# Delta rule of a three-part block: value columns ahead of gate columns, half of the decay factors made early

## The reference

```
qkv = x @ w_qkv;  z = x @ w_z;  beta = sigmoid(x @ w_b)
g = -exp(a_log) * softplus(x @ w_a + dt_bias)
qkv = silu(causal depthwise conv of 4 taps(qkv))     # q, k: 16 heads, v: 32 heads of 128
q, k = l2norm(q) * 128 ** -0.5, l2norm(k)
g = cumsum(g) within the chunk of 64
decay[i, j] = exp(g[i] - g[j]) for i >= j, else 0
A = -(beta * k) @ k.T * decay, strictly lower
attn = inverse(I - A);  v_new = attn @ (beta * v)
o = (q @ k.T * decay) @ v_new
out = (o * rsqrt(mean(o * o) + eps) * norm_w * silu(z)) @ w_out
```

## Time and profile before

| | us |
|---|---|
| median of 3 runs (lowest to highest) | 2776.75 (2775.61 to 2778.75) |
| the profiled execution, its own time | 2778.05 |
| its span | 2776.3 |
| projection columns 32 to 95 in it | 1970 to 2194 |
| groups in it | 2194 to 2362 |

### The profile page before, as it was taken

The page is one execution under the profiler, slowest core; times in us unless marked ns, Lnnn a source line. Parts: engine busy times, 40 slices in busy tenths (PEclk is TensorE's granted clock), DMA queues, the critical chain, the costliest instruction groups (busy, mean ns, idle before and its releaser), DMA issues.

```text
span 2776.3 us, 38769 instructions
## 1 busy us (share of the span) xinstructions
PE 2639.8 (95%) x13810; PEld 2192.9 (79%) x13810; DVE 1766.5 (64%) x3857; ACT 1529.8 (55%) x2992; POOL 502.1 (18%) x428
## 2 busy tenths in 40 slices
PE   6879999999999999999999999999999879998999
PEld 5668788888887887887887887878777669777887
DVE  7855636546546546546455466668669866668997
ACT  7944435435435435445444355437686567856776
POOL 4402102002002012011011020015353332022111
PEclk9989999999999999999999999999999999999999
DMA  3533013022022021030030121435675642549996
GB/s 126 137 98 104 18 43 104 11 61 85 15 77 65 20 85 49 24 94 30 27 100 16 40 85 48 149 123 162 171 214 168 155 95 67 187 186 366 377 372 226
DMA packets 255054, 317.85 MB, mean 114 GB/s; under 512 B 128712, under 2 KB 166216, under 8 KB 241808
## 3 DMA queue, kind: packets, MB, share of 16 engines
q1 hardware_dynamic: 251392, 310.03, 35.3%
q0 software_dynamic: 3040, 5.08, 0.7%
q10 hardware_dynamic: 432, 0.27, 0.0%
HBM read 274.22 MB, written 46.98 MB: 116 GB/s over the span
## 4 chain that ended last, share of the span: by engine, by line
PE 80%; DVE 10%; ACT 3%; DMA 2%; issue 2%; SPq 1%; POOL 1%; POOLq 0%; DVEq 0%; ACTq 0%
PE ps L103 21%; PE ps L105 21%; PE ps L104 21%; PE ps L887 3%; PE ps L843 3%; PE ps L915 2%; DVE lnw L2171 2%; DVE zz L2174 2%; PE ps L868 2%; DVE cv L2138 1%; PE ps L908 1%; PE ps L1346 1%; PE ps L1345 1%; PE ps L2012 1%; ACT qn L380 1%
## 5 line engine op out<-in xcount | busy, mean ns | idle before, releaser
L1246 POOL TENSOR_TENSOR lnw<-lnw,half 128x8 f32<-128x8 f32 x88 | 144.4, 1641 | 1202.4 <-DVE lnw L981 1202.4
L103 PE MATMUL ps<-whf,cth 128*128 128x512 f32 (+1 forms) x832 | 335.9, 404 | 0.0
L103 PE MATMUL ps<-cnh,pth 128*128 128x512 f32 (+1 forms) x832 | 330.1, 397 | 1.4 <-issue 1.4
L105 PE MATMUL ps<-whf,ctl 128*128 128x512 f32 (+1 forms) x832 | 325.9, 392 | 0.0
L104 PE MATMUL ps<-wlf,cth 128*128 128x512 f32 (+1 forms) x832 | 325.5, 391 | 0.0
L104 PE MATMUL ps<-cnl,pth 128*128 128x512 f32 (+1 forms) x832 | 324.9, 390 | 0.0
L105 PE MATMUL ps<-cnh,ptl 128*128 128x512 f32 (+1 forms) x832 | 324.7, 390 | 0.0
L2664 DVE TENSOR_TENSOR ml<-mr,mh 128x2048 fp32r<-128x2048 f32 x90 | 203.3, 2287 | 26.6 <-ACT mh L2606 26.6
L1157 ACT ACTIVATE pr<-ps,sm 128x1601 f32<-128x1601 f32 x56 | 89.7, 1601 | 210.0 <-DVE sm L1023 210.0
L1182 ACT ACTIVATE xo<-ps 128x128 f32<-128x128 f32 x64 | 17.8, 278 | 312.7 <-PE ps L915 312.7
L1042 DVE TENSOR_TENSOR ptl<-ps,pth 128x512 fp32r<-128x512 f32 (+1 forms) x256 | 139.1, 585 | 79.0 <-ACT pth L1169 78.6
(11 more groups left out here) (352 smaller groups left out, 6398.4 us busy)
## 6 DMA issues: line engine op xcount, KB each, us to landing
mr<-in_moe SPq DMA_DIRECT2D x90, 1024.0 KB, 7.0
ctr<-in_ctxt SPq DMA_DIRECT2D x96, 256.0 KB, 2.7
pr<-in_ctxn SPq DMA_DIRECT2D x96, 256.0 KB
wv<-in_wv SPq DMA_DIRECT2D x64, 256.0 KB, 2.8
wr<-in_wqkv SPq DMA_DIRECT2D x64, 256.0 KB, 2.9
wvf<-in_wattn SPq DMA_DIRECT2D x11, 1024.0 KB, 5.1
ca<-cat_d SPq DMA_DIRECT2D x16, 512.0 KB, 3.9
qk_d<-cv SPq DMA_DIRECT2D x32, 256.0 KB, 3.2
```

The source lines that it names most:

```text
L103: pe.matmul(dst, lh, rh, start=first, stop=False)
L105: return pe.matmul(dst, ll, rh, start=False, stop=last)
L1246: po.tensor_tensor(rs[0:w, s, :], nv[0:w, s, :], half[0:w, 0:8], ALU.pow).then_inc(kx_rs, 1)
```

## The change

Columns 32 to 63 are now all values and columns 64 to 95 all gates. The decay factors of builds 16 to 31 are made in four rounds among columns 54 to 89, each for 16 rows of the gate table: eight broadcast loads into the tile pg, mask and gate added by GpSimd, one exponential, then products with beta and with the norm of q by GpSimd, and a store of both to cf_d. The loads of these builds fetch the factors, so their "build" has no step on GpSimd and no "decay", and "second" makes the coupling by two smaller products (L2243, L2245 of the changed kernel). Since the factors hold the norm, groups from 16 on are evicted without a scale. The gate table in DRAM has three planes (with the norm) and lies in halves. The first solve has larger budgets (columns 63 to 76), the second starts at 81 and ends by 93. The clearing of mt and xt moves from column 38 to 91, behind the last store of factors. Squares start at t = 8 at half the pace, with two per step from 24 on; those from group 8 on are one operation on ScalarE and a reduction on VectorE. Who evicts which group stays as it was.

```diff
-        gb_d = dram("gb_d", [128, 2, 128])
+        gb_d = dram("gb_d", [2, 128, 3, 64])
+        cf_d = dram("cf_d", [4, 128, 2048])
...
-        gT = sb5g("gT", [128, 2, 128])
+        gT = sb5g("gT", [128, 3, 128])
         s5g.close()
+        s5p = ExitStack()
+        pg = stack_sb(s5p)("pg", [128, 16, 3, 64])
+        s5p.close()
...
-        OUT_AC = 20
...
+        ALONE = 8
+
+        def on_ac(n):
+            return n < 20
...
-        GATE_PLACES, VALUE_PLACES, place = [], [], 32
-        for k in range(32):
-            if k not in (6, 12, 18, 24):
-                GATE_PLACES.append(place)
-                place += 1
-            VALUE_PLACES.append(place)
-            place += 1
-        GATE_PLACES += list(range(place, NPOS))
+        VALUE_PLACES, GATE_PLACES = list(range(32, 64)), list(range(64, NPOS))
...
-                yield "decay", n, 0
...
+                k, r = divmod(s - 54, 9)
+                if 0 <= k < 4:
+                    if r < 2:
+                        yield "pg_load", k, 2 * r
+                        yield "pg_load", k, 2 * r + 1
+                    if r in (3, 4):
+                        yield "pg_mask", k, r - 3
+                    if r == 5:
+                        yield "pg_exp", k, 0
+                    if r in (6, 7):
+                        yield "pg_scale", k, r - 6
+                    if r == 8:
+                        yield "pg_store", k, 0
+                if s == 91:
+                    yield "clear", 0, 0
...
-                if 63 <= s < 83:
-                    yield from some(steps, 170 if burst < 4 and 4 <= r < 8 else 800)
-                if s == 83:
+                if 63 <= s < 76:
+                    yield from some(steps, 600 if burst < 4 and 4 <= r < 8 else 1300)
+                if s == 76:
                     yield from steps
-                if s == 84:
                     yield "solved", 0, 0
+                if s == 79:
                     yield "system", 1, 0
                     steps = solving(1)
-                if 88 <= s < NPOS:
-                    yield from some(steps, 700 if s < 92 else 2000)
+                if 81 <= s < 93:
+                    yield from some(steps, 1100)
+                if s == 93:
+                    yield from steps
+                    yield "solved", 1, 0
...
-            squares, fetched, solved_to = 0, 3, 0
+            squares, fetched, solved_to = 0, 3, 1
             for t in range(36):
                 if t < 32:
                     yield "p0", t, 0
-                yield from some(steps, 400 if t < 3 else 700)
+                yield from some(steps, 500 if t < 12 else 700)
                 if 0 <= t - 1 < 32:
                     yield "p1", t - 1, 0
-                for _ in range(2 if t < 3 else 1):
+                for _ in range(2 if t < 4 else 1):
                     if todo:
                         yield from building(todo.pop(0))
-                if t == 13:
+                if t == 12:
                     yield from built()
                 if 0 <= t - 2 < 32:
                     yield "p2", t - 2, 0
-                yield from some(steps, 400 if t < 3 else 800 if t < 15 else 1000)
+                yield from some(steps, 400 if t < 12 else 800)
                 if 0 <= t - 3 < 32:
                     yield "p3", t - 3, 0
-                if t in (4, 14, 22):
+                if t in (14, 22):
                     yield from steps
-                    solved_to = (4, 14, 22).index(t) + 1
+                    solved_to = (14, 22).index(t) + 2
                     yield "solved", solved_to, 0
-                if t in (6, 15):
-                    steps = solving(2 if t == 6 else 3)
+                if t in (5, 16):
+                    steps = solving(2 if t == 5 else 3)
                 while fetched < 16 and 2 * fetched <= t + 3 and fetched // 4 <= solved_to:
                     yield "fetch", fetched, 0
                     fetched += 1
-                if t in (5, 14):
+                if t in (4, 14):
                     yield "system", solved_to + 1, 0
                 if t >= 2 and t % 2 == 0 and t // 2 + 1 < 16:
                     yield "fetch_coupling", t // 2 + 1, 0
-                if squares <= t - 4 and squares < 28:
-                    yield "square", squares, 0
-                    squares += 1
-                    if squares % 2 == 0:
-                        yield "rms", squares // 2 - 1, 0
+                for _ in range(2 if t >= 24 else 1 if 8 <= t and t % 2 == 0 else 0):
+                    if squares < 28:
+                        yield "square", squares, 0
+                        squares += 1
+                        if squares % 2 == 0:
+                            yield "rms", squares // 2 - 1, 0
...
+            if m >= 8:
+                sp.wait_ge(*d_cf.at(16 * ((m - 8) // 2 + 1)))
             for b in range(2):
-                sp.dma_start((gb2 if core_over(m) else gb)[64 * b:64 * b + 64, f:f + 2, :, :, :].rearrange("p f h a t -> p (f h) a t"),
-                             gb_d[8 * m:8 * m + 8, :, 64 * b:64 * b + 64].unsqueeze(0).to_broadcast([64, 8, 2, 64])).then_inc(d_gb[m % 4].sem, 16)
+                dst = (gb2 if core_over(m) else gb)[64 * b:64 * b + 64, f:f + 2, :, :, :]
+                if m >= 8:
+                    sp.dma_start(dst.rearrange("p f h a t -> p (f h a t)"),
+                                 cf_d[(m - 8) // 2, 64 * b:64 * b + 64, 1024 * (m % 2):1024 * (m % 2) + 1024]).then_inc(d_gb[m % 4].sem, 16)
+                else:
+                    sp.dma_start(dst.rearrange("p f h a t -> p (f h) (a t)"),
+                                 gb_d[b, 8 * m:8 * m + 8, 0:2, :].rearrange("h a t -> h (a t)").unsqueeze(0).to_broadcast([64, 8, 128])).then_inc(d_gb[m % 4].sem, 16)
+
+        def factor_load(sp, k, part):
+
+            sp.wait_ge(d_gt, 32)
+            if k > 0:
+                sp.wait_ge(*d_cf.at(16 * k))
+            h, row = 4 * part, 64 + 16 * k + 4 * part
+            for b in range(2):
+                sp.dma_start(pg[64 * b:64 * b + 64, h:h + 4, :, :].rearrange("p h a t -> p (h a t)"),
+                             gb_d[b, row:row + 4].rearrange("h a t -> (h a t)").unsqueeze(0).to_broadcast([64, 768])).then_inc(d_pg.sem, 16)
+
+        def factor_store(sp, k):
+            sp.wait_ge(*pg_scaled.at(4 * k + 4))
+            sp.dma_start(cf_d[k].rearrange("p (h c) -> p h c", h=16),
+                         pg[:, :, 0:2, :].rearrange("p h a t -> p h (a t)")).then_inc(d_cf.sem, 16)
...
-                    sp.dma_start(gb_d, gT[:, :, :]).then_inc(d_gt, 16)
+                    for b in range(2):
+                        sp.dma_start(gb_d[b], gT[:, :, 64 * b:64 * b + 64]).then_inc(d_gt, 16)
...
+                elif step == "pg_exp":
+                    ac.wait_ge(*pg_masked.at(8 * n + 8))
+                    ac.activation(pg[:, :, 0, :], pg[:, :, 0, :], ACT.Exp).then_inc(pg_exp.sem, 1)
...
+                    if n < 16:
+                        for q in range(4):
+                            f = ac.activation(vb[:, j, h + q, :], bank(3 + n % 5)[:, 128 * q:128 * q + 128], ACT.Copy,
+                                              scale=rq[:, j, h + q:h + q + 1])
+                    else:
+                        f = ac.activation(vb[:, j, h:h + 4, :], bank(3 + n % 5).rearrange("p (h d) -> p h d", h=4), ACT.Copy)
...
-                    ac.wait_ge(*apD_out.at(n + 1))
+                    ac.wait_ge(*group_out(n))
                     if n >= 3:
                         ac.wait_ge(*sso_out.at(n - 2))
                     else:
                         ac.wait_ge(*d_gz[n].at(16 * (11 if n < 2 else 10)))
-                    for h in range(4):
-                        hd = 4 * (n % 8) + h
-                        f = ac.activation(gz[:, n % 3, 128 * h:128 * h + 128], vb[:, n // 8, hd, :], ACT.Square,
-                                          accum_out=sso[:, n // 8, hd:hd + 1])
-                    f.then_inc(sso_out.sem, 1)
+                    hd = 4 * (n % 8)
+                    if n < ALONE:
+                        for h in range(4):
+                            f = ac.activation(gz[:, n % 3, 128 * h:128 * h + 128], vb[:, n // 8, hd + h, :], ACT.Square,
+                                              accum_out=sso[:, n // 8, hd + h:hd + h + 1])
+                        f.then_inc(sso_out.sem, 1)
+                    else:
+                        ac.activation(gz[:, n % 3, :].rearrange("p (h d) -> p h d", h=4), vb[:, n // 8, hd:hd + 4, :],
+                                      ACT.Square).then_inc(o_squared.sem, 1)
...
-                elif step == "start":
-                    po.wait_ge(d_gt, 16)
+                elif step == "pg_mask":
+                    e = pg[:, 8 * k:8 * k + 8, 0, :]
+                    po.wait_ge(*d_pg.at(128 * (n + 1)))
+                    po.tensor_tensor(e, e, negm.unsqueeze(1).to_broadcast([128, 8, 64]), ALU.add).then_inc(pg_masked.sem, 2)
+                    m = 4 * n + 2 * k
```

(42 more changed lines are left out.)

36 lines of the change are left out of this document (24 added, 12 removed).

## The result

The changed kernel takes **2808.5 us** (median of 4 runs, 2806.8 to 2810.9) against 2776.2 for the kernel before on the same chip (2774.0 to 2778.8, 4 runs): ratio 1.0120, 95% interval 1.0108 to 1.0133. It is slower by 1.2%; the forecast was 2769 with a range up to 2786. The profiled execution took 2809.1 us with a span of 2807.3. Three executions of the experiments' sets that took 5240 to 9297 us are left out of the ratios.

What follows compares the result with a forecast made beforehand. VectorE was taken to bound the stretches where TensorE waits. Groups starting 14 us later and 21 us removed from them gave -7 on 2778.05, 2771; less 1.3 and rounding, 2769, range 2750 to 2786.

Steps and rivals of the forecast that it cites:

- Value part, +2: Value columns 32 to 63: VectorE keeps up, ScalarE comes near TensorE's pace; 2 us, from 0 to 6.
- Order and VectorE's load, columns to 2187 without locks and seam: Gate columns: two solves, splits, taps and `second`s on VectorE make TensorE wait 9 us beyond 2176.
- floor of 2176: End of the columns if TensorE waits for nothing, from the present 2194.1 less waits and lower-clock time.
- Locks, +18: Gate columns: 28.2 us of GpSimd work beside two solves holds VectorE up at 0.65, 18 us, all reaching TensorE.
- Rivals 1 and 2: GpSimd's rounds don't block VectorE, 2751, chance 0.24; or all 28.2 us of GpSimd are lost to VectorE, 2779, chance 0.12.
- The transfers, +0: Columns: the forecast's sum has no term for the bytes that the factor rounds move.
- rival 3: Columns: SyncE's queue bounds, factor loads waiting for the former round's store, chunk loads behind: +15, 2784, chance 0.14.
- Seam, +3: Columns to groups: clearing mt and xt waits for the last factor store, delaying fetch and eviction; 3 us, 0 to 6.
- Groups, -21: Delta rule groups: second solve gone, less GpSimd and ScalarE work, fewer waits and less low clock; 21 us removed.
- The fetch of the fourth system 1.2 becomes 2: Groups: TensorE's wait at the fetch of the fourth solved system grows from 1.2 to 2 us.
- Rival 4: Groups give little, as TensorE waits for chains of latencies: 15 us less gained, 2784, chance 0.05; sign, over 160 us.

Runs made afterwards that it cites:

- order alone: Kernel before with only the new column order and the first two solves' new budgets, no factor rounds: 2782.2 us, ratio 1.0014 to 1.0036.
- six slots: Changed kernel with six slots instead of three for the gate columns' results, three of them in cv: 2808.6 us, ratio 1.0103 to 1.0137.

## Why the prediction was wrong

The direction, the size and the range all failed: 2769 forecast, 2808.5 measured. The step that failed most is one term that was put at nothing, the bytes of the factor rounds; the order of columns, the seam and the groups were mis-sized as well. By its steps:

- **Value part, +2.** Right: TensorE was idle 3.3 of its 115 us, and ScalarE, which was to come near TensorE's pace, busy 99.4.
- **Order and VectorE's load, columns to 2187 without locks and seam.** The order alone came to 2198.7, 12 us later. TensorE was idle 18.0 us in its columns from 1970 on (228.0 less 209.95 busy) where the prediction's 9 and 2 make 11. Some 4 of the rest are in the floor of 2176, which leaves 206 us for TensorE's own work where it was busy 210. The forecast had a gain of 7 from the new distribution; it cost 5.
- **Locks, +18.** Right in kind and near in size: VectorE lost some 17 us in the gate columns, at an estimated 0.65 per us of GpSimd as forecast, and the columns 12.3, or 15.8 with the transfers out of the way (352.2 less 336.4). Rivals 1 and 2 are both out.
- **The transfers, +0.** This is the step that failed. "Against: where VectorE lags, SyncE is not the last" dismissed rival 3 by asking who comes last in SyncE's queue. The runs showed 13.8 us for the bytes of three rounds, or 17.3 with GpSimd's work out of the way (353.7 less 336.4); the stands themselves, rival 3's mechanism, gave 3.3 back when removed. The sum of bytes per column was never made, though the prediction's own rows have the column times. Rival 3 let 1.6 MB move in 3 us, which is over 500 GB/s, where no stretch of the columns shown here moved more than 303. It also let a chunk load be some 8 us late, though each waits for one of three slots first. The rings of gz and wr then turn late landings into late high parts.
- **Seam, +3.** 5.9 us at the first p0, at the upper end of the 0 to 6 it was given; the order alone had 0.8 there.
- **Groups, -21.** 9.6 measured. Up to the 24th group the forecast held: the 21st p0 came 95.0 us after the first, before 112.9, so 17.9 less, and the 24th 106.5, before 126.9. "The fetch of the fourth system 1.2 becomes 2" was 6.9; at the 25th group 13.2 were left. But the fetch alone is not the cause, as the solves made earlier took that wait away and gave back 0.7. The last stretch gave back 3.6 more, 2.8 of it because TensorE was busy 37.6 us with the 308 matmuls it does there in place of 34.8, at a granted clock of 0.95 in place of 1.00. Rival 4 (over 160 us) is out by 2 us only, less than the 5 by which the groups scatter.

In the sum, the columns lost 38.7 against 14 forecast: 12 of the difference are the order's, some 14 the transfers', 2 to 3 the seam, with the locks 2 to 6 under the forecast. The groups add 11. That these parts come so near the whole is in part luck, as the locks and the transfers each come out 3.5 us dearer when the other is out of the way. Against the order alone, the factors cost 33.3 us in the columns and gave 9.0 back in the groups (166.8 less 157.8); even at the 21st group they were ahead by only 17.2 (112.2 less 95.0).

What stays open: how the 12 us of the order's shortfall divide between splits made too late and the gz ring, as the six slots took only 2.4 of them; whether the rounds' bytes cost by rate or by later landings; what of the groups' gain is the factors', and why the earlier solves gave nothing; and whether the factors' volume would be cheaper in another form, which wasn't tried.

## What to carry to other kernels

Before gathering columns of one kind, add up the bytes per us that they want from the DMA engines, with every store and every new transfer, and compare it with the mixture before (here some 299 against 133 GB/s). Then ask how many slots each transfer has: here, with three, landings later by 1 to 2 us came with longer waits of the engines. A high share of the DMA engines is not yet a loss; the changed kernel's last stage had 1.00 with TensorE busy 70.0 of 70 us. The longest pieces of the chain of waits name what was last, not what is dear; only the kernel without the wait tells (here 3.3 us for 14.5% of the chain). The same holds for a single wait of TensorE: taking 6.7 us of it away gave 0.7. And widening one ring may only uncover the next.

## What the runs showed of the hardware

- VectorE's operations on two SBUF tiles lost about 0.65 us (an estimate from the two traces) for each us of GpSimd operations taken away, 24 operations of 512 elements; the mean of a 128x512 split rose from 724 to 927 ns.
- In 2110 to 2200 us of the change, with a share of the DMA engines of 0.93 and 0.94 in its last 60 us, transfers of 256 KB took 4.6 to 5.0 us to land (median), with six slots 4.5 to 5.3; with the order alone it was 3.3 to 3.6 and in the kernel before 2.8 to 3.2.
- The core moved 286 to 303 GB/s at a share of 0.94 to 0.97 in the columns, and 375 at 1.00 in the last stage with loads of 1024 KB.
- Two 64 KB stores issued beside other traffic took 5.3 us, three in another kernel 3.1, two of 1024 KB 8.0.
- The gains from leaving out GpSimd's operations and the transfers added up (26.1 us singly, 29.6 together), though VectorE's splits were what TensorE waited for in both.
